# One attention-plus-feed-forward kernel: the exponentials' arguments come from a transfer and a ScalarE bias instead of a matmul and a VectorE minimum

## The reference

```
logfg = log_sigmoid(f_pre)
Fcum  = cumsum(logfg, axis=-1)
Dmat  = Fcum[..., :, None] - Fcum[..., None, :] + i_pre[..., None, :]
Dmat  = where(causal, Dmat, -inf)
m     = max(Dmat, axis=-1, keepdims=True)
Smat  = exp(Dmat - m)
C     = (q @ k^T / sqrt(dqk)) * Smat
n     = maximum(abs(sum(C, -1)), exp(-m))
h     = (C / n) @ v
```

## Time and profile before

| | |
|---|---|
| time before, median of 3 | 2454.16 us (2453.58 to 2456.21) |
| the profiled execution, its own time | 2458.68 us |
| its span in the trace | 2456.9 us |
| mean granted TensorE clock | 0.994 |
| start of unit 0's exponents, SECOND and the six looped halves | 156.6, 371.7, 581.6, 796.8, 1006.7, 1223.0, 1432.9 us |

### The profile page before, as it was taken

The page is one execution under the profiler, slowest core; times in us unless marked ns, Lnnn a source line. Parts: engine busy times, 40 slices in busy tenths (PEclk is TensorE's granted clock), DMA queues, the critical chain, the costliest instruction groups (busy, mean ns, idle before and its releaser), DMA issues. The chain is left out here.

```text
span 2456.9 us, 33428 instructions
## 1 busy us (share of the span) xinstructions
PE 2397.4 (98%) x11488; PEld 1951.4 (79%) x11488; DVE 1264.5 (51%) x2233; ACT 855.6 (35%) x1459; POOL 609.0 (25%) x499
## 2 busy tenths in 40 slices
PE   7999999999999999999999999999999999999998
PEld 5678778788887887888787888888888888888887
DVE  6777546765773675577467657743122222222222
ACT  5433244354353435444434534454111111111111
POOL 2346423221321322232032223222111111111111
PEclk9899999999999999999999999999999999999999
DMA  5166575475566648556555755675867867867865
GB/s 211 48 215 235 214 274 182 169 275 193 185 209 222 202 164 286 185 189 216 204 190 187 276 184 176 238 259 206 294 240 272 286 236 255 302 239 250 294 218 199
DMA packets 179141, 545.17 MB, mean 222 GB/s; under 512 B 17392, under 2 KB 74736, under 8 KB 143760
## 3 DMA queue, kind: packets, MB, share of 16 engines
q1 hardware_dynamic: 158400, 518.50, 60.3%
q10 hardware_dynamic: 20560, 24.39, 3.0%
HBM read 439.41 MB, written 102.37 MB: 221 GB/s over the span
## 5 line engine op out<-in xcount | busy, mean ns | idle before, releaser
L795 PE MATMUL gate_bank<-act_hi,gud 128*128 128x512 f32 x1728 | 574.7, 393 | 2.6 <-DVE th L1656 2.6
L795 PE MATMUL up_bank<-act_hi,gud 128*128 128x512 f32 x1728 | 571.7, 392 | 0.0
L2158 POOL TENSOR_TENSOR hidden_lo<-hm,hidden_hi 128x512 fp32r<-128x512 f32 x216 | 282.0, 1306 | 1121.6 <-ACT hidden_hi L1189 1121.6
L1005 PE MATMUL acc<-gud,hidden_hi 128*128 128x512 f32 x1728 | 438.9, 396 | 0.9 <-ACT hidden_hi L1189 0.9
L1656 DVE SCALAR_TENSOR_TENSOR th<-th,gate_bank 128x512 f32<-128x512 f32 x216 | 147.9, 685 | 515.7 <-ACT th L1184 515.6
L795 PEld LDWEIGHTS gate_bank<-act_hi,gud 128*128 128x128 f32 x1728 | 324.4, 188 | 75.0 <-DVE th L1656 4.5
L1189 ACT ACTIVATE hidden_hi<-hm 128x512 fp32r<-128x512 f32 x216 | 135.9, 629 | 708.4 <-PE acc L1008 696.7
L795 PEld LDWEIGHTS up_bank<-act_hi,gud 128*128 128x128 f32 x1728 | 324.6, 188 | 65.7
L1005 PEld LDWEIGHTS acc<-gud,hidden_hi 128*128 128x128 f32 x1728 | 321.1, 189 | 68.7 <-issue 4.1
L795 PE MATMUL gate_bank<-act_lo,gud 128*128 128x512 f32 x864 | 336.8, 390 | 0.0
L795 PE MATMUL up_bank<-act_lo,gud 128*128 128x512 f32 x864 | 336.2, 389 | 0.0
(11 more groups left out here) (331 smaller groups left out, 2911.1 us busy)
## 6 DMA issues: line engine op xcount, KB each, us to landing
gud<-mlp_parts SPq DMA_DIRECT2D x112, 1024.0 KB, 5.0
gud<-ghost_parts SPq DMA_DIRECT2D x88, 1024.0 KB, 5.2
gud<-mlp_parts SPq DMA_DIRECT2D x112, 512.0 KB, 3.8
gud<-ghost_parts SPq DMA_DIRECT2D x88, 512.0 KB, 4.1
stack<-qk_parts SPq DMA_DIRECT2D x336, 64.0 KB, 2.0
ghost_parts<-look_w SPq DMA_DIRECT2D x35, 512.0 KB, 3.6
mlp_parts<-gud SPq DMA_DIRECT2D x16, 1024.0 KB, 3.9
vo_w_hi<-vo_parts SPq DMA_DIRECT2D x13, 1024.0 KB, 7.3
```

Of the source, the lines that this page charges most:

```text
L795: mm = pe.matmul(dst, l[a], r[c], start=first and k == 0 and n == 0, stop=last and k == len(lhs) - 1 and n == 2)
L1005: pe.matmul(ACC[i][:], HH[0][:, toks(i)], W3[:, z, 2, n, :], start=t == 0 and n == 0, stop=False)
L2158: pool.tensor_tensor(HH[1][:], hm[:], HH[0][:].bitcast(f32), ALU.subtract).then_inc(of.low.sem, 1)
```

## The change

The matmul of exponents and the minimum go away. The running maxima (8 rows of 512) are stored to DRAM (`store_max`, one transfer for a half) and loaded again for each block, spread over all 128 partitions (`load_max`, 512 KB, issued from ScalarE's queue). GpSimd adds a mask of +10000 above the diagonal (`mq_`). ScalarE forms exp(-1 x tile + bias) with one instruction for each head, whose bias is the column of the keys' exponents; those columns come out of `factors`, whose rows grow from 72 to 104. Scores and the state's part of the output now share bank B, the values and the state's update bank A. In `tiles`, ScalarE takes the unit's exponentials ahead of `tanh`. The maxima for blocks 2 and 3 are loaded in tiles 1 and 3 and masked in tiles 2 and 4. TensorE does `unit_3` of unit 0 in tile 1, after gate.

```diff
-                pe.matmul(pick(at, u, A, ACC[0])[:], AL[:, toks(j)], MX[:, g * HG:(g + 1) * HG, :], start=True, stop=True)\
-                    .then_inc(pe_unit.sem, 1)
...
                 if u:
-                    wait(pe, vec_unit, at, u - 1, "update")
+                    wait(pe, vec_unit, at, u - 1, "before")
...
             def unit_3(at, u):
-                wait(pe, vec_unit, at, u, "before")
+                wait(pe, vec_unit, at, u, "heads")
...
-                        fill[u, 2] = [(unit_3, u)]
+                        fill[u, 2] = [(unit_3, u)] if u else []
+                    fill[1, 0].insert(0, (unit_3, 0))
...
+            def store_max(at):
+                wait(act, vec_rows, at, 0, "max")
+                act.dma_start(max_rows.rearrange("j h n -> h j n"), mx[:, 1:].rearrange("h (j n) -> h j n", j=NB))\
+                    .then_inc(st_max, 16)
+
+            def load_max(at, j):
+                if j == 0:
+                    act.wait_ge(st_max, at[0] * (HALVES * 16) + (at[1] * 16 + 16))
+                elif j >= 2:
+                    wait(act, act_unit, at, 2 * j - 3, "exp")
+                act.dma_start(mq[:, j % 2, :, :], max_rows[j].unsqueeze(0).to_broadcast([P, H, P]))\
+                    .then_inc(ld_max[j % 2], 16)
...
             def unit(at, u):
-                wait(act, vec_unit, at, u, "masked")
+                j, g = u // G, u % G
+                wait(act, pool_mq, at, j)
...
-                act.activation(pick(at, u, ex, ex2)[:, :, :], pick(at, u, ar, ar2)[:, :, :], ACT.Exp).then_inc(act_unit.sem, 1)
+                c = j * RW + 96 + g * HG
+                for h in range(HG):
+                    ins = act.activation(pick(at, u, ex, ex2)[:, h, :], mq[:, j % 2, g * HG + h, :], ACT.Exp,
+                                         bias=rn[:, c + h:c + h + 1], scale=-1.0)
+                ins.then_inc(act_unit.sem, 1)
...
-                    tanh(MLP, mb, t, stage)
                     if stage and t < UNITS:
                         unit(at, t)
+                        if t in (1, 3):
+                            load_max(at, t // 2 + 2)
+                    tanh(MLP, mb, t, stage)
...
-                dve.tensor_tensor(pick(at, u, ar, ar2)[:, :, :],
-                                  pick(at, u, A, ACC[0])[:].rearrange("p (h n) -> p h n", h=HG),
-                                  maskd[:].unsqueeze(1).to_broadcast([P, HG, P]), ALU.min)\
-                    .then_inc(vec_unit.sem, 1)
...
+            def mq_(at, j):
+
+                pool.wait_ge(ld_max[j % 2], max_loaded(at, j))
+                pool.tensor_tensor(mq[:, j % 2, :, :], mq[:, j % 2, :, :], maskd[:].unsqueeze(1).to_broadcast([P, H, P]),
+                                   ALU.add).then_inc(pool_mq.sem, 1)
...
                 if stage and not here(at, SECOND):
-                    mx_(at, 0)
+                    mq_(at, 0)
+                    mq_(at, 1)
...
-                        if t in (1, 3, 5):
-                            mx_(at, t // 2 + 1)
+                        if t in (2, 4):
+                            mq_(at, t // 2 + 1)
```

More of the change, by code:

```diff
@@ L327, in program @@
         look_vec = sem("look_vec")
+        st_max = sem("st_max")
+        ld_max = [sem(f"ld_max{i}") for i in range(2)]
         st_x1 = sem("st_x1")
@@ L348, in program @@
         pe_o = Steps(sem("pe_o"), NB, ["done"])
-        pe_unit = FirstAhead(sem("pe_unit"), UNITS, ["exponents", "scores", "values", "state"], 2, credit=1)
+        pe_unit = FirstAhead(sem("pe_unit"), UNITS, ["scores", "values", "state"], 1, credit=1)
         pe_hoT = Steps(sem("pe_hoT"), NB, ["done"])
@@ L363, in program @@
         act_xT = Steps(sem("act_xT"), NB, ["hi"], ahead=NB)
-        ROWS = ["natural", "summed", "scaled", "biased", "m0", "g0", "cum", "a", "a_hi", "a_lo", "max", "m_hi", "m_lo",
-                "inter", "keys", "bound", "carry", "factors"]
+        ROWS = ["natural", "summed", "scaled", "biased", "m0", "g0", "cum", "a", "max", "inter", "keys", "bound", "carry", "factors"]
         vec_rows = Steps(sem("vec_rows"), 1, ROWS)
@@ L369, in program @@
         vec_qkT = Steps(sem("vec_qkT"), NB, ["lo"], credit=-NB)
-        vec_unit = FirstAhead(sem("vec_unit"), UNITS, ["masked", "weights", "before", "heads", "update", "state"], 1)
+        vec_unit = Steps(sem("vec_unit"), UNITS, ["weights", "before", "heads", "update", "state"])
         vec_norm = Steps(sem("vec_norm"), NB, ["size", "floor", "inverse", "divided", "squares", "sums", "mean", "scaled", "gated"])
@@ L479, in ho_bank @@
         def ho_bank(at, i):
-            return A if not here(at, FIRST) else UB if i < NB - 1 else GB
+            return B if not here(at, FIRST) else UB if i < NB - 1 else GB
         def pj_bank(at, n):
@@ L877, in unit_1 @@
                 if u:
-                    wait(pe, vec_unit, at, u - 1, "update")
+                    wait(pe, vec_unit, at, u - 1, "before")
+                if u % 2 and u >= 3:
+                    wait(pe, vec_hoT, at, u // 2 - 1, "lo")
                 for h in range(HG):
@@ L1311, in gate_rows @@
                 act.activation(rows(at)[1], UB[32:40, :], ACT.Copy).then_inc(act_gates.sem, 1)
-            def a_high(at):
-                wait(act, vec_rows, at, 0, "a_hi")
-                act.activation(AL[64:64 + H, :], ah(at).bitcast(f32), ACT.Copy).then_inc(act_gates.sem, 1)
             def exps(at):
                 wait(act, vec_rows, at, 0, "bound")
-                for r in range(0, RW, 32):
+                for r in range(0, 96, 32):
                     act.activation(rwe[r:r + H, :], rows(at)[3][r:r + H, :], ACT.Exp).then_inc(act_gates.sem, 1)
+                act.activation(rwe[96:96 + H, :], rows(at)[2], ACT.Copy).then_inc(act_gates.sem, 1)
+            def store_max(at):
[9 more added lines that the diff above has]
+                    .then_inc(ld_max[j % 2], 16)
             def qk(at, i):
@@ L1391, in front @@
                 qkT_(at, 3)
-                a_high(at)
                 store_qk(at, 3)
                 v(at, 1)
+                store_max(at)
                 v(at, 2)
                 exps(at)
+                for j in range(2):
+                    load_max(at, j)
                 if here(at, FIRST):
@@ L1419, in unit @@
             def unit(at, u):
-                wait(act, vec_unit, at, u, "masked")
+                j, g = u // G, u % G
+                wait(act, pool_mq, at, j)
                 if u == 0:
                     wait(act, pe_gates, at, 0, "factors")
-                act.activation(pick(at, u, ex, ex2)[:, :, :], pick(at, u, ar, ar2)[:, :, :], ACT.Exp).then_inc(act_unit.sem, 1)
+                    wait(act, vec_rows, at, 0, "factors")
+                ahead = 2 if here(at, FIRST) else 1
+                if u >= ahead:
+                    wait(act, vec_unit, at, u - ahead, "weights")
+                c = j * RW + 96 + g * HG
[3 more added lines that the diff above has]
+                ins.then_inc(act_unit.sem, 1)
             def ho_T(at, i):
@@ L1434, in units_first @@
                 qbd_(FIRST, 0)
+                unit(FIRST, 0)
                 qbd_(FIRST, 1)
                 for u in range(UNITS):
-                    unit(FIRST, u)
+                    if u + 1 < UNITS:
+                        unit(FIRST, u + 1)
+                    if u in (1, 3):
+                        load_max(FIRST, u // 2 + 2)
                     if u in (4, 5, 6, 7):
@@ L1748, in gate_maxima @@
                 wait(dve, vec_rows, at, 0, "max")
[L1750 to L1754, removed]
             def gate_factors(at):
@@ L1819, in factor @@
                 return rn[:, c:c + hs].unsqueeze(2).to_broadcast([P, hs, width])
[L1821 to L1837, removed]
-                dve.tensor_tensor(pick(at, u, ar, ar2)[:, :, :],
-                                  pick(at, u, A, ACC[0])[:].rearrange("p (h n) -> p h n", h=HG),
-                                  maskd[:].unsqueeze(1).to_broadcast([P, HG, P]), ALU.min)\
-                    .then_inc(vec_unit.sem, 1)
             def weights(at, u):
+                if u == 0 and not here(at, FIRST):
+                    chunk_stored(dve, at, 2)
+                    chunk_stored(dve, at, 3)
                 wait(dve, act_unit, at, u, "exp")
```

80 lines of the change are left out of this document (21 added, 59 removed).

## The result

| | before | after |
|---|---|---|
| median | 2455.36 us (2450.3 to 2458.7, 16 runs) | 2461.39 us (2458.5 to 2463.9, 16 runs) |
| ratio after/before | | 1.0023, 95% interval 1.0016 to 1.0030 |
| the profiled execution, its span | 2458.68, 2456.9 us | 2458.79, 2457.0 us |

The changed kernel is slower by 0.23%, about 0.0023 x 2455 = 5.6 us. The forecast had +3.3 us, a time of 2457.5 on a base of 2454.16, which more runs put at 2455.4. The two profiled spans agree to 0.1 us, so here a comparison of spans says nothing: single executions of one kernel differ by several us, partly where the loop over sequences turns round (138.5 and 140.3 us from the last unit of one sequence to the first of the next in this trace, with a mean granted clock of 1.00 and 0.99, and 135.7 from SECOND, against 134.7 within a sequence).

A forecast was written before the change was run, and what follows sets the result against it. TensorE, busy 98% of the span, was taken as the bound. Looped halves +4.4, SECOND -0.1 and FIRST -1.0 gave +3.3 us on 2454.16, so 2457.5 us, with a range of 2444 to 2467 to hold 8 in 10.

The forecast's parts named there:

- The queue on ScalarE: Looped halves, tiles 3, 5, 7: four exponentials ahead of tanh delay `unit_2`, +1.48, +1.40, +0.74, sum +3.62 us a half.
- Exponents: Looped half on TensorE: all eight exponent matmuls go, 0.23 us each, -1.84 us.
- rival C: Scores' weights still wait at the same place, so -1.84 shrinks to about -1 a half: 2462 us, chance 0.05.
- `front`: Start of a looped half: four rows go, TensorE's wait goes (-0.74), extra ScalarE work costs +0.10, together -0.64 us.
- wider factors: Looped half: the wider rows of `factors` add four times 32 columns, taken as +0.1 us.
- Tile 0: Looped half: moving `unit_3` of unit 0 behind the next gate removes TensorE's wait of up to 0.6 us, -0.60 us.
- queued behind `down`, which covers it: Looped half: `unit_3` waits for `heads`, 0.43 us behind `before`, hidden by `down`; only GpSimd's add in tile 4 costs +0.1.
- A looped half: Sum of the terms for one looped half: +0.74 us, for six +4.4.
- SECOND: SECOND's tiles: exponents -1.84, tile 0's wait about -0.5, mask add delaying VectorE +1.8, tiles 4 and 6 +0.4: -0.1 us.
- FIRST: FIRST: exponents -2.4 over seven units, a second add delaying VectorE's scaling at its end +1.4, together -1.0 us.
- Rival A: Stalls do not appear because ScalarE's queue has unseen room: a looped half gives -2.9, time 2436 us, chance 0.18.
- Rival B: Start of a half: maxima arrive late, about 1.5 us a half, +9 in all, 2466 us, chance 0.17.

The follow-up runs named there:

- experiment 1: Changed kernel with the exponentials of units 3, 5 and 7 formed one tile earlier, block 3's load moved along: 2436.62 us, ratio 0.9921 to the kernel before.
- experiment 2: Changed kernel with tanh ahead of the four exponentials in tiles 3, 5 and 7, block 3's load behind them: 2449.28 us, ratio 0.9970 to the kernel before.
- experiment 4: Changed kernel with one exponential a unit instead of four with a bias each, leaving out the keys' exponents: 2446.76 us, ratio 0.9958 to the kernel before.
- experiment 3: Changed kernel with only the issue of block 3's load moved behind tanh in tile 3: 2460.72 us, ratio 1.0022 to the kernel before.
- experiment 6: Kernel before with only the state matmuls of unit 0 moved into tile 1: 2453.03 us, ratio 0.9989 to the kernel before.
- experiment 5: Changed kernel with the state matmuls of unit 0 put back in tile 0: 2468.65 us, ratio 1.0052 to the kernel before.
- experiment 7: Changed kernel with FIRST's GpSimd mask addition for block 3 moved behind the factors of unit 4: 2459.73 us, ratio 1.0018 to the kernel before.
- experiment 8: Changed kernel with exponentials of units 3, 5, 7 one tile earlier and FIRST's block 3 addition later: 2435.81 us, ratio 0.9915 to the kernel before.

## Why the prediction was right, and where not

The time lay in the range and the forecast was the case that came. By its own steps:

- **The queue on ScalarE** was right, mechanism and size, in the looped halves. With a first exponent's 0.23 off each tile, its +1.48, +1.40 and +0.74 make distances that grow by 1.25, 1.17 and 0.51; they grew by 1.27, 1.16 and 0.51. Experiments 1, 2 and 4 show the cause by removing it, halving it and repricing it, experiment 3 the part of the issue.
- **Exponents** off TensorE: the distances from 1 to 2, 3 to 4 and 5 to 6 are 0.21, 0.14 and 0.21 shorter for a forecast of 0.23 each; rival C falls.
- **`front`**: -0.64 and the exponents of unit 0, together -0.87; with the +0.1 for wider factors -0.77. The distance from unit 7 to the next unit 0 within a sequence fell by 135.49 - 134.69 = 0.80.
- **Tile 0**: forecast -0.83, measured -0.85, but by two errors that cancel. The -0.60 for the move was sized on a wait that the move alone does not remove (experiment 6: -0.28), and "queued behind `down`, which covers it" is not so in tile 0, where no `down` stands (experiment 5: +0.50 by the exchange, then -1.12 by the move).
- **A looped half** in all: forecast +0.74, measured 75.87 - 74.37 - 0.80 = +0.70, for six +4.2 against +4.4.
- **SECOND**: forecast -0.1, measured -1.2 from unit 0 to unit 7 (75.71 to 74.53). The mechanism was right: VectorE's second multiply takes 2.77 us beside the mask's addition, and the state waits for `hr`. It was mis-sized by tile: the distance from 2 to 3 grew by 0.25, where +1.8 for tile 2 less an exponent's 0.23 were forecast, and the one from 4 to 5 by 1.14, where +0.4 stood for tiles 4 and 6 together. What was missing are the distances from 3 to 4 and 5 to 6, each 0.76 shorter and not 0.23. Before, TensorE stood idle for 0.31 us in front of the scores in both, waiting for the state's update in bank B; with the banks exchanged that wait is gone. That explains part of it. That the meeting with the addition is the cost is borne out by experiment 1, where it is missed and 2.1 us go; the other distances of SECOND no experiment took apart.
- **FIRST** was mis-sized, and one term of it was missing: forecast -1.0, measured +1.7 from its unit 0 to SECOND's (90.70 to 92.40; the same distance in the traces of experiments 1 to 5 lies between 91.8 and 94.8). From unit 3 on the units gave 0.05 to 0.25 each, less than the 0.34. The term that is not in the sum at all is one more collision, the addition for block 3 beside the product into `kv`: +1.5 in the gap from 2 to 3, shown by experiment 7. The second addition at FIRST's end was taken at +1.4; the scaling took 2.59 for the 2.11 of the earlier trace rows, +0.5, and the subtraction behind it (1.51) was off the path. TensorE's wait for the scaling was 1.19 before and is 1.63 or 1.64 in experiments 3, 7 and 8; in the trace of the kernel after it is not there, because the projections ahead of it ran at the lower clock (a mean of 0.57 from 144 to 148), which took the same time. What was left out there is that `unit_3` of unit 7 waits for `hr` with nothing in front: 1.18 us, where the earlier trace rows have at most 0.6 for `tt`.
- **Rival A** came nowhere near: the stalls are there. Its price of 2436 is, by the numbers, what experiment 1 reaches once they are gone. **Rival B** falls: the maxima are ready before anybody asks.

The sum of the measured pieces is 4.2 - 1.2 + 1.7 = +4.7 us, against 5.6 with an interval of 3.9 to 7.4. That the forecast's +3.3 came so near is in part luck: it had SECOND 1.1 us too high and FIRST 2.7 us too low.

Nor do the pieces close the account. Three things are not in them. The way from SECOND's unit 7 to the first looped half fell from 139.45 to 135.66 us, where 0.80 is counted; it takes 139.4 in both traces of the kernel before (one of them with the move of experiment 6) and 135.6 to 138.8 in the eight of the changed kernel and its variants. The start of FIRST's unit 0 is at 69.3 and 67.7 us in the former, and between 69.2 and 71.2 in the latter. And the mean granted clock is 0.9938 over the 16 runs of the kernel after and 0.9956 over 37 runs of the kernel before. By the 1.0 us for 0.001 of experiment 3 this is 1.8 us, which the forecast did not have; whether the change itself lowers the clock, and by what, stays open.

The Trainium skill, SBUF — State Buffer (Who interferes with whom), was weighed in the prediction for the second addition. Its rule, that a VectorE operation with two SBUF inputs and a GpSimd operation that reads SBUF exclude each other, agrees with the two products here (0.43 us became 2.60, 0.69 became 2.77). The scaling of `first_rows` is not of that form, with one tensor input and a scalar column, and was held up too (2.59 us, where the same instruction takes 0.48 with no addition beside it), once and not twice: it ran beside the first addition and ended as the second was beginning.

## What to carry to other kernels

Before moving work to an engine that is a third busy, look at its queue just ahead of the instruction that the bottleneck waits for. Here 1.2 to 1.7 us in front of tanh, in three tiles of sixteen, cost more than all that was taken off TensorE (3.5 us against 3.1 in a looped half), and the same instructions one tile earlier cost nothing there and made a loss of 0.2% a gain of 0.8%. Give work whose inputs are ready early to the gap in which its engine waits, not to the tile that uses it. And count edits of banks and of order together: one of them alone can be worth a quarter, or less than nothing.

## What was not expected of the hardware

A short VectorE product of two SBUF tiles takes six times as long beside a GpSimd addition over 128x1024, 2.60 us for 0.43; it ends 0.3 us after the addition. One such meeting cost TensorE 1.5 us where the weights of a unit are queued behind it.

TensorE's clock can fall to its lower level for some us in two of six halves that have the same work and the same waits, which costs 1.6 us each time (experiment 3). An edit worth 3 us in the trace distances can be lost in that. So compare the granted clock of all runs too, and not only the distances of one trace: here it differs by 0.001 to 0.003 between the kernels.
